# First scores by the head and second scores by pairs of heads, in the second attention of a two-layer network

## The reference, cut to what matters

```python
c_k = x @ w_dk + b_dk;  c_v = x @ w_dv + b_dv
k = c_k @ w_uk + b_uk;  v = c_v @ w_uv + b_uv
q, k = rope(heads(x)), rope(heads(k))
attn = softmax(einsum('bhid,bhjd->bhij', q, k) / sqrt(8))
x = layernorm(x + (attn @ heads(v)) @ w_o + b_o)
```

## Time and profile before

| What | Value |
|---|---|
| Median of 3 runs | 2001.37 us (1997.99 to 2001.47) |
| Profiled execution, its own time | 2002.48 us |
| Its span | 2000.7 us |
| Mean granted TensorE clock | 0.848 |
| TensorE busy | 1576.0 us, 79% |
| VectorE busy | 1241.4 us, 62% |
| ScalarE busy | 950.0 us, 47% |
| GpSimd busy | 641.5 us, 32% |

### The profile page before, as it was taken

One profiled execution on the slowest core, in us unless ns is written; L12 is line 12 of the kernel. 1 busy time (PEld: TensorE's weight loads), 2 busy tenths in 40 slices (PEclk: granted clock), 3 DMA queues, 4 the chain that ended last, 5 costly groups with the idle time before them and its releaser, 6 DMA issues. The chain is left out here.

```text
span 2000.7 us, 36805 instructions
## 1 busy us (share of the span) xinstructions
PE 1576.0 (79%) x11187; PEld 1165.8 (58%) x11188; DVE 1241.4 (62%) x3388; ACT 950.0 (47%) x2383; POOL 641.5 (32%) x818
## 2 busy tenths in 40 slices
PE   6999989999899669994126877777777758888887
PEld 4777767777677558884014545454554436555654
DVE  4776666667666546664555555555555457666766
ACT  4655656566555335552012434343333335566655
POOL 1344444444444300003841111011111035554555
PEclk9999999999999879997556767676667669999998
DMA  4102101021010011111120000000000000000000
GB/s 154 54 19 64 64 17 58 21 68 58 16 58 21 11 34 46 47 46 37 45 62 4 4 7 4 6 7 3 7 3 3 0 16 6 5 5 5 5 5 10
DMA packets 45459, 55.18 MB, mean 28 GB/s; under 512 B 7716, under 2 KB 39500, under 8 KB 44148
## 3 DMA queue, kind: packets, MB, share of 16 engines
q1 hardware_dynamic: 40900, 45.76, 7.2%
q0 software_dynamic: 4096, 8.40, 1.4%
q10 hardware_dynamic: 432, 0.66, 0.1%
HBM read 43.57 MB, written 30.08 MB: 37 GB/s over the span
## 5 line engine op out<-in xcount | busy, mean ns | idle before, releaser
L998 POOL TENSOR_TENSOR m_hid<-m_act_out,m_wb 128x512 f32<-128x512 f32 x132 | 190.3, 1455 | 192.9 <-ACT m_act_out L905 106.5
L360 POOL TENSOR_TENSOR a_prob<-a_prob,a_rl 128x128 f32<-128x128 f32 (+1 forms) x258 | 125.4, 507 | 313.3 <-DVE a_rl L442 312.9
L244 ACT ACTIVATE a_prob<-psum,a_nmx 128x128 f32<-128x128 f32 (+1 forms) x516 | 212.6, 424 | 11.8 <-DVE a_nmx L437 11.8
L1977 DVE TENSOR_REDUCE a_mx<-psum 128x4 f32<-128x1024 f32 x136 | 166.6, 1225 | 78.3 <-PE psum L1701 78.3
L1059 DVE TENSOR_TENSOR m_hid_l<-m_hid,m_hid_h 128x512 fp32r<-128x512 f32 x162 | 143.0, 888 | 114.4 <-ACT m_hid_h L919 110.2
L1701 PE MATMUL psum<-a_stk 32*128 32x256 f32 x544 | 95.6, 442 | 99.2 <-DVE a_mx L1977 98.3
L274 ACT ACTIVATE a_probt<-psum 128x768 f32<-128x768 f32 x128 | 103.8, 811 | 143.1 <-PE psum L625 143.1
L1853 ACT ACTIVATE a_prob<-psum 128x1024 f32<-128x1024 f32 x128 | 129.3, 1023 | 39.1 <-PE psum L1720 39.1
L1701 PEld LDWEIGHTS psum<-a_stk 32*128 32x128 f32 x544 | 61.0, 273 | 143.3 <-DVE a_mx L1977 140.8
L625 PE MATMUL psum<-ident,a_prob 128*128 128x128 f32 x768 | 110.5, 282 | 41.8 <-DVE a_prob L446 41.8
L1471 POOL DMA_INDIRECT c_rows<-ys,idx x64 | 62.5, 976 | 244.8 <-SPq L1463 227.3
(11 more groups left out here) (310 smaller groups left out, 4588.9 us busy)
## 6 DMA issues: line engine op xcount, KB each, us to landing
xs<-in_zeros SPq DMA_DIRECT2D x72, 256.0 KB, 3.9
a_stage<-in_w SPq DMA_DIRECT2D x16, 384.0 KB, 4.0
m_xrow<-xs SPq DMA_DIRECT2D x71, 64.0 KB, 1.8
ys<-m_yrow SPq DMA_DIRECT2D x71, 64.0 KB, 1.6
a_stage<-in_w SPq DMA_DIRECT2D x16, 160.0 KB, 2.2
out<-m_nrm SPq DMA_DIRECT2D x9, 256.0 KB, 2.2
a_xin<-in_x SPq DMA_DIRECT2D x17, 128.0 KB, 2.1
xs<-a_nrm,a_idx POOLq DMA_INDIRECT x64
```

The lines of the kernel that those rows point to most:

```text
L244: last = nc.scalar.activation(prob[:, slot, h, at], S[:, 2 * slot + h, at], ACT.Exp, bias=nmx[:, slot, q, h:h + 1], accum_out=lsum[:, slot ...
L360: last = nc.gpsimd.tensor_tensor(prob[:, slot, 0, at], prob[:, slot, 0, at], rl[:, slot, 0, q:q + 1].to_broadcast(prob[:, slot, 0, at].sha ...
L998: nc.gpsimd.tensor_tensor(hid[:, w % D, :], act_out[:, w % 2, :], wb[:, w // FB, :], ALU.mult).then_inc(prod_done, 1)
L1977: nc.vector.reduce_max(mx[:, :, 2 * u:2 * u + 2].rearrange("p q h -> p h q"), g.psum[:, 4:6, :].rearrange("p h (q k) -> p h q k", q=QB), A ...
```

## The change: what it does

First scores are now issued one head at a time: the even heads go to R0, the odd ones to R1, 2 matmuls each, and head h waits only until the maxima of head h - 2, which used the same bank, are done. The maxima are taken over one bank, 128 x 512, 16 times a pass, and `s1_ps` and `mx_done` count heads.

Second scores are issued by pairs of heads: pair t uses banks 2 (t mod 2) and 2 (t mod 2) + 1 of `ST`, 8 matmuls on two bands, and waits for exponential t - 2. There are eight in a pass, and each exponential waits for its own pair. The bands of rows are kept.

The order on TensorE is written anew around the eight pairs. Pair 0, `tail_heads`; pair 1, `values`, `tail_columns`; pair 2, `tail_project`, stacks 0 and 1, outputs(0); pair 3, stacks 2 and 3, `tail_rows`; pair 4, outputs(1), heads 0 to 3 of the first scores; heads 4 and 5, pair 5, heads 6 and 7, `tail_store`; heads 8 and 9, pair 6, heads 10 and 11, outputs(2); heads 12 and 13, pair 7, heads 14 and 15. On VectorE `normalise` stands behind head 3 and `tail_store` behind head 11. `negate` is rewritten with shorter names only, but for the count that it waits for.

```diff
--- before.py
+++ after.py
@@ -1688,19 +1688,17 @@
                         last = nc.tensor.matmul(out, sel[:, 2 * j + 1, k, :], qk_l[:, j, :], start=False, stop=True)
                     last.then_inc(stack_ps, 1)
 
-            def first_scores(u, p, n):
-
-                if u == 0:
+            def first_scores(h, p, n):
+
+                if h == 0:
                     pe.wait_ge(stack_act, n * 2)
                     pe.wait_ge(stack_dve, n * 2)
-                else:
-                    pe.wait_ge(mx_done, n * NPR + (u - NPR))
-                for q in range(QB):
-                    for h in (2 * u, 2 * u + 1):
-                        j, at = h % HG, slice(q * P, (q + 1) * P)
-                        last = nc.tensor.matmul((R0, R1)[h % 2][:, q * T:(q + 1) * T], stk[band(j), p, h // HG, at],
-                                                stk[band(j), p, h // HG, T:2 * T], start=True, stop=True,
-                                                tile_position=(32 * j, 0))
+                if h >= 2:
+                    pe.wait_ge(mx_done, n * H1 + (h - 1 - H1))
+                for q in range(QB):
+                    j = h % HG
+                    last = nc.tensor.matmul((R0, R1)[h % 2][:, q * T:(q + 1) * T], stk[band(j), p, h // HG, q * P:(q + 1) * P],
+                                            stk[band(j), p, h // HG, T:2 * T], start=True, stop=True, tile_position=(32 * j, 0))
                 last.then_inc(s1_ps, 1)
 
             def maxima(n):
@@ -1710,15 +1708,16 @@
                     last = nc.tensor.transpose(R0[:, q * P:(q + 1) * P], mh[:, q, :].bitcast(F32), g.ident[:])
                 last.then_inc(mt_ps, 1)
 
-            def scores(k, p):
-
-                for c in range(QB):
-                    for j in range(HG):
-                        nc.tensor.matmul(ST[:, j, c * T:(c + 1) * T], stk[band(j), p, k, T + c * P:T + (c + 1) * P],
-                                         stk[band(j), p, k, 0:T], start=True, stop=False, tile_position=(32 * j, 0))
-                    for j in range(HG):
-                        last = nc.tensor.matmul(ST[:, j, c * T:(c + 1) * T], pick[band(j), k * HG + j, :], mt[band(j), :],
-                                                start=False, stop=True, tile_position=(32 * j, 0))
+            def scores(t, p):
+
+                heads = [(h, h % HG, ST[:, 2 * (t % 2) + h % 2, :]) for h in (2 * t, 2 * t + 1)]
+                for k in range(QB):
+                    for h, j, out in heads:
+                        nc.tensor.matmul(out[:, k * T:(k + 1) * T], stk[band(j), p, h // HG, T + k * P:T + (k + 1) * P],
+                                         stk[band(j), p, h // HG, 0:T], start=True, stop=False, tile_position=(32 * j, 0))
+                    for h, j, out in heads:
+                        last = nc.tensor.matmul(out[:, k * T:(k + 1) * T], pick[band(j), h, :],
+                                                mt[band(j), :], start=False, stop=True, tile_position=(32 * j, 0))
                 last.then_inc(st_ps, 1)
 
             def outputs(k, p, n):
@@ -1773,8 +1772,8 @@
             values(1)
             pe.wait_ge(sel_done, 1)
             stacks(range(NGR), 1)
-            for u in range(NPR):
-                first_scores(u, 0, 1)
+            for h in range(H1):
+                first_scores(h, 0, 1)
             pe.wait_ge(v_done, 1)
             pe.wait_ge(ksin_done, 1)
             latents(columns_of(1), 2)
@@ -1784,38 +1783,40 @@
                 for p in range(2):
                     n = i * 2 + p
                     ahead, behind = columns_of(n + 2), columns_of(n - 1)
-                    for k in range(NGR):
-                        if k == 0:
+                    for t in range(NPR):
+                        if t == 0:
                             pe.wait_ge(mt_done, n + 1)
                             pe.wait_ge(v_done, n + 1)
-                        if k >= 1:
-                            pe.wait_ge(exp_done, n * NPR + 2 * k)
-                        scores(k, p)
-                        if k == 0:
-                            tail_heads(n + 1)
-                            values(n + 2)
-                            tail_columns(n + 1)
-                        if k == 1:
+                        if t >= 2:
+                            pe.wait_ge(exp_done, n * NPR + t - 1)
+
+                        if t >= 5:
+                            for h in range(4 * t - 16, 4 * t - 14):
+                                first_scores(h, 1 - p, n + 2)
+                        scores(t, p)
+                        if t == 2:
                             tail_project(behind, n + 1)
                             pe.wait_ge(rt_done, n + 1)
                             stacks((0, 1), n + 2)
-                            outputs(0, p, n)
+                        if t == 4:
+                            outputs(1, p, n)
+                        if t >= 4:
+                            for h in range(4 * t - (16 if t == 4 else 14), 4 * t - 12):
+                                first_scores(h, 1 - p, n + 2)
+                        if t in (2, 6):
+                            outputs(t // 2 - 1, p, n)
+                        if t == 0:
+                            tail_heads(n + 1)
+                        if t == 1:
+                            values(n + 2)
+                            tail_columns(n + 1)
+                        if t == 3:
                             pe.wait_ge(v_done, n + 2)
                             pe.wait_ge(ksin_done, n + 2)
                             stacks((2, 3), n + 2)
                             tail_rows(n + 1)
-                        if k == 2:
-                            first_scores(0, 1 - p, n + 2)
-                            first_scores(1, 1 - p, n + 2)
-                            outputs(1, p, n)
-                            first_scores(2, 1 - p, n + 2)
-                        if k == 3:
-                            first_scores(3, 1 - p, n + 2)
+                        if t == 5:
                             tail_store(n + 1)
-                            first_scores(4, 1 - p, n + 2)
-                            outputs(2, p, n)
-                            for u in range(5, NPR):
-                                first_scores(u, 1 - p, n + 2)
                     pe.wait_ge(nt_done, n + 1)
                     latents(ahead, n + 3)
                     maxima(n + 2)
@@ -1847,8 +1848,7 @@
                 nc.scalar.activation(stk[:, p, k, :], R0, ACT.Copy).then_inc(stack_act, 1)
 
             def exps(t, n):
-                if t % 2 == 0:
-                    act.wait_ge(st_ps, n * NGR + t // 2 + 1)
+                act.wait_ge(st_ps, n * NPR + t + 1)
                 k = t // 2
                 nc.scalar.activation(prob[:, k % 2, 2 * (t % 2):2 * (t % 2) + 2, :], ST[:, 2 * (t % 2):2 * (t % 2) + 2, :],
                                      ACT.Exp, scale=SCALE).then_inc(exp_done, 1)
@@ -1972,21 +1972,19 @@
                 dve.wait_ge(stack_ps, n * NGR + (k + 1 - NGR))
                 nc.vector.tensor_copy(stk[:, p, k, :], R1).then_inc(stack_dve, 1)
 
-            def maxima(u, n):
-                dve.wait_ge(s1_ps, n * NPR + (u + 1 - NPR))
-                nc.vector.reduce_max(mx[:, :, 2 * u:2 * u + 2].rearrange("p q h -> p h q"),
-                                     g.psum[:, 4:6, :].rearrange("p h (q k) -> p h q k", q=QB), AX.X).then_inc(mx_done, 1)
+            def maxima(h, n):
+                dve.wait_ge(s1_ps, n * H1 + (h + 1 - H1))
+                nc.vector.reduce_max(mx[:, :, h:h + 1], (R0, R1)[h % 2].rearrange("p (q k) -> p q k", q=QB), AX.X
+                                     ).then_inc(mx_done, 1)
 
...
@@ -2054,11 +2052,12 @@
                     stacks(1, 1 - p, n + 2)
                     stacks(3, 1 - p, n + 2)
                     variances(n + 1)
-                    for u in range(NPR):
-                        maxima(u, n + 2)
-                        if u == 1:
+                    for t in range(4, NPR):
+                        for h in range(4 * (t - 4), 4 * (t - 3)):
+                            maxima(h, n + 2)
+                        if t == 4:
                             normalise(n + 1)
-                        if u == 4:
+                        if t == 6:
                             tail_store(columns_of(n - 1), n + 1)
                     negate(n + 2)
             chain.end(B // 2)
```

More of the change, by code:

```diff
@@ L1973, in stacks @@
                 nc.vector.tensor_copy(stk[:, p, k, :], R1).then_inc(stack_dve, 1)
-            def maxima(u, n):
-                dve.wait_ge(s1_ps, n * NPR + (u + 1 - NPR))
-                nc.vector.reduce_max(mx[:, :, 2 * u:2 * u + 2].rearrange("p q h -> p h q"),
-                                     g.psum[:, 4:6, :].rearrange("p h (q k) -> p h q k", q=QB), AX.X).then_inc(mx_done, 1)
+            def maxima(h, n):
+                dve.wait_ge(s1_ps, n * H1 + (h + 1 - H1))
```

(20 more changed lines are left out.)

## The result

| What | Before | After |
|---|---|---|
| Median, both measured on one chip | 2000.96 us (4 runs, 1997.99 to 2001.47) | 2074.34 us (4 runs, 2055.97 to 2081.75) |
| Profiled execution, its span | 2002.48, 2000.7 | 2072.64, 2070.8 |
| Second attention | 512.4 us, clock 0.71 | 590.3 us, clock 0.61 |
| Mean granted clock of the run | 0.848 | 0.819 |

The ratio is 1.0356 with a 95% interval of 1.0288 to 1.0425: slower by 3.6%. The forecast was 2055, in a range of 1996 to 2125, with 0.70 on slower.

A forecast was written before the change was run, and what follows sets the result against it. TensorE's order of work, fed by VectorE in the middle, was taken to end each pass. Terms summed to -0.1 us a pass, 2001 us; six lost rises at 9 us added 54, giving 2055, range 1996 to 2125.

The forecast's parts named there:

- Direction and mechanism: Second attention: two-band scores before the clock's rise lose late rises; 0.70 on slower by over 0.2%.
- Number of lost rises: Head of the pass: the six late rises of 16 passes are lost, +54 us; six to seven likeliest (0.30).
- rival C: Second attention: misses follow each other, most rises lost, 13 passes x 9 = 117 us, 2118 us; chance 0.25.
- Price of a low head: A pass without its rise: head at 1.2 GHz costs 7.9 us, middle 0.9 more, 9 us a pass.
- A kept pass: Pass with the clock as it is: +2.4 - 4.4 + 1.3 - 0.4 + 1.0 = -0.1 us.
- The round of the maxima: Middle, VectorE and TensorE: two heads every 1.57 us instead of 2.12 at the low clock, saving 0.55 us a pair.
- the stand before the store: Middle: VectorE waits 2 us for ScalarE's xth before storing, where it lost 0.96; 1.0 us more a pass.
- 4.4 us for eight rounds: Middle: alternating banks for first scores and maxima save 0.55 us a pair of heads, 4.4 us a pass.
- A: Second attention, balance: the rises stay, 2001 us, 1993 to 2009; chance 0.22.
- B: Middle: denser work keeps or restores the high clock, 2.6 us a pass, 1960 us, or 1988 in a third; chance 0.11.
- D: Middle: lone band fills slowly or bank released late, two heads cost 2.1 us as before, +69, 2070 us; chance 0.10.
- E: Middle: the change does not take effect, first scores still in step with the maxima, 2001 us; chance 0.02.

The follow-up runs named there:

- the split in the kernel before: Kernel before, with group 0 of the second scores split: bands 0 and 1 before the transposes of the heads, bands 2 and 3 behind; 2032.78 us, 1.0166.
- The first half alone: Kernel before, with only first scores and maxima one head at a time on two banks, second scores still in groups of four; 1978.08 us, 0.9886.
- Three kernels with middles of 15.5 and 15.0 us: Kernel before with single-head first scores and maxima, 1978.08 us; plus ScalarE copying xth before outputs(2), 1977.83; plus outputs(2) behind heads 10 and 11, 1977.17.

## Why the prediction was right, and where it was off

**Direction and mechanism: right.** I expected TensorE's clock to stay low in some passes because half the bands work in the run before the rise. The signs that I named are there: first scores 20 us after the start in low passes and 12 in the others, passes of 40 to 41.5 and of 32 with one between (37.8), maxima of 0.68 us that start 0.79 us apart for each head at the low clock and 0.64 at the high one (four in 2.58 us), a stand of 2.06 us before the store. That work on four bands instead of two is the cause is shown by the kernel with bands 2 and 3 beside pair 0 (2074 to 2001 us at equal time at work; rows or the number of matmuls, it doesn't tell), and that the split is enough by the split in the kernel before (+32 us). My evidence for the step was weaker than I made it: of the stretch of 11.37 us at 0.50, the second half, from 1622.63 to 1628.20, was full matmuls, busy all the time and at 0.50 too. Those rows don't tell rows from time; the run with bands 2 and 3 does. The Trainium skill (TensorE: Matmul & The Clock Gate, "What's actually happening") has the gate follow how busy the engine has been. Read as time, the traces don't agree: 7.13 of 7.30 us busy, and the clock stayed at 0.50.

**Number of lost rises: mis-sized, and the step behind it was wrong.** I counted six, the late ones of the earlier trace rows. Nine were lost, and they are other passes: before, the late ones were 1, 4, 7, 9, 12 and 14. Whether a rise is late is no property of a pass; each low pass is 8 us longer and moves all that comes after it. The runs vary too, from 2056 to 2082 us. That is a part of rival C, which had misses follow each other (7 and 8, 10 and 11 do), but not in a row through the stage. Three more at 8 us are 24 us, more than the whole miss of 19. The kept passes (below) add some 7 us to what I had, and the cheaper low heads and what stands ahead of the loop take some 9 off, so that the sum came this close is in part luck.

**Price of a low head: right.** Where the clock did not rise at all, the head gave 20.46 - 11.75 = 8.7 us and the middle 0.6; I had 9 in all. Where it rose at 19 us, in five of the nine, the pass cost 7.9 more, and that is also the mean.

**A kept pass: -0.1 expected, +0.3 measured** (32.32 against 32.00, means of all). Head: +2.4 expected; 11.75 for 9.61, with the rise at the same place, is +2.1, and +1.8 in the mean. Middle: 14.47 for 16.05 is -1.6 (-1.5 in the mean) instead of -2.5. The round of the maxima is right where TensorE does nothing else (0.55 us less for two heads at the low clock), and so is the stand before the store (2.06, I said 2). What failed is the sum over the middle, and the kernel with pairs and the old maxima divides it. Pairs and outputs(1) together were to cost 1.3 - 0.4 = 0.9 us, and the middle went from 16.05 to 15.9. Single heads on top were to give 4.4 less 1.0 for the store, 3.4, and it went from 15.9 to 14.5, only 1.4. The mis-sized term is thus "4.4 us for eight rounds", by 2 us, and the charge for the pairs hid half of that. The first half alone says the same, where 4.4 gave 0.5: there VectorE waits 2.05 us for the store and 1.14 for scores behind group 3, so short rounds end in other waits.

**Left out.** The 16 first scores ahead of the loop also run on two banks. From the first of them to the first copy of `mt` it took 14.0 us after and 18.3 before, -4.3, which is close to 8 x 0.55. I had charged the loop alone.

**The rivals.** A (2001) and B (faster) fell by the clock, though A is what the changed kernel would have been with its rises: the kernel with bands 2 and 3 beside pair 0, in the same order and as long at work, is at 2001, and the one with group 0 on four bands at 1994. C (13 passes) fell in its number, with nine. D fell: the banks overlap, 1.57 us for two heads. E fell: `L1977` runs 16 times a pass, each over 512 columns.

## What to carry to other kernels

Where TensorE's clock rises and falls once in every pass, look at what it does just before the rise, and keep all row bands at work there: splitting one group of four bands cost more than the rest of the change could earn. Try the parts of a change one at a time: here one half is worth -22 us and the other costs +65. And a shorter round on one engine is worth only what is not waiting behind it, and, where the passes run in step with the clock, not even that.

## What was not expected of the hardware

**Matmuls on other bands start ahead of earlier ones.** In the kernel with group 0 in pairs, bands 2 and 3 started with bands 0 and 1 although eight matmuls stood before them in the code, and so did pair 1 behind pair 0 (x4 in both timelines). The Trainium skill (TensorE: Matmul & The Clock Gate, "Step-by-step: what each phase is for") says that matmuls stay in program order and only weight loads are pulled ahead; for matmuls on different row bands these traces show otherwise. So what is said ahead of the prediction, that an engine does its instructions in the order in which they stand, does not hold on TensorE between bands. The transposes on all rows were not passed: in the changed kernel's third pass they start at 1139.54 us and pair 1 at 1141.44.

**Narrow matmuls hide beside other bands.** Four matmuls on band 0 behind outputs(3) lengthened the tail by 0.39 us, four on all rows by 1.16. In the fourth pass's tail the next pair's score on band 1 starts at 1211.31 us, ahead of two of the four added on band 0 (1211.42 and 1211.54), and the one on band 0 behind them at 1211.65. What either filler gives back in the clock is not clear from these runs.

**The pass settles.** Three kernels with middles of 15.5 and 15.0 us came to the same 30.73 us a pass, as long as one cycle of the clock, 13.65 us high and 17.07 low. Why the cycle keeps that length is open.
